# Sending every second-product unit down as fp16 halves in a four-layer attention and mixture kernel

## The chip, the cores and the metric

The program runs on one core of one Trainium2 chip. The metric is device time in microseconds (us) of one execution; three timed executions of the kernel before are given below, and one more execution was profiled.

## The reference

Sixteen samples of 128 rows by 128 features go through four residual layers; each begins with a layer norm (the second and third norms of the list below are of the running `x`).

```python
x = x + _L0_xattn_ref(_layernorm(x), ctx)          # A: softmax(x ctx^T) ctx, one head
x = x + _L0_ffn_ref(_layernorm(x), ...)            # B: 16-head attention, q/k/v weights mixed from 4 experts (top 2)
x = x + _L1_xattn_ref(_layernorm(x), ctx, ...)     # C: 16-head cross attention with rotary positions, 77 keys
x = x + _L1_ffn_ref(_layernorm(x), ...)            # D: causal 16-head attention, then a mixture of 8 experts:
#   y = x + layernorm(attn) * g + b
#   w = softmax over the top 2 of y @ gate_W, spread over 8 experts
#   h = relu(y @ W1[e] + b1[e])        W1[e]: 128 x 512
#   moe = sum_e w[e] * (h @ W2[e] + b2[e])   W2[e]: 512 x 128
#   out = y + layernorm(moe) * g2 + b2'
```

All eight experts are computed for every row and weighted.

## The kernel before

Two samples at a time are a job; there are eight jobs, numbered 0 to 7. A job's layers A to D up to the router run in one of five lanes (jobs 0, 5 in lane 0; 1, 6 in lane 1; 2, 7 in lane 2; 3 and 4 in lanes 3 and 4). The mixtures of experts run in a sixth lane, one job after the other, and a seventh does the splitting of the weights ahead of the first of them. `ORDER` is a string written out by hand of a planner: each digit is a lane that takes its next step, and all five engines walk this one list of steps in this order, each doing its own share of a step. Every engine is thus an in-order queue: an instruction that waits holds up all that stands behind it on its engine. `TAKEN` gives the PSUM bank of each use.

The mixture of a job has 32 units: a unit is 128 of the 4096 hidden columns, four units to an expert. Two units are a piece, so 16 pieces make a job. The step `moe` of piece n does on TensorE the upward product of its two units (three fp16 matmuls each: high weight by high and low input, low weight by high input, L743 to L745), then the downward products of piece n-2 (`down`); on ScalarE two ReLUs of 128x256 from PSUM into the ring `hT` of six units in fp32 (L889). The step `halve` makes fp16 halves of the odd unit alone: VectorE copies `hT` to fp16 (L1108) and GpSimd subtracts to get the low half (L1202); in job 7 (`LATE`) VectorE subtracts too (L1111). Downward, the even unit is multiplied in fp32 (L681) and the odd unit by three fp16 products (L690, L694). Every second expert, `take_up` adds a finished expert's product to `acc`, weighted (L1019).

When a job's mixture is through, VectorE takes moments, GpSimd makes the scales (`moe_end`), ScalarE normalises, GpSimd multiplies and adds twice (`moe_out`, L1213, L1215), and the store goes out. The next job's mixture starts with `moe_start` (L734), which needs that job's router weights: the logits (`D.lg`), six GpSimd instructions that rank them (L1148 to L1155), VectorE's `top`, the transpose `D.cT` (L608) and its copy (L1013). The first product upward needs `ylo` too, which GpSimd makes at the step `top` (L1205).

In each of the 24 attention layers the step `M` finds the maximum of every row and head: four reduces from PSUM into `negmax` (L1088), and after the second sample two more VectorE instructions that split it into an fp16 value and an fp16 remainder, side by side in `m8` (L1092, L1093). The step `mt` turns `m8` by TensorE, and `E` adds it to the scores by a matmul with the constant `two`, which takes up both columns; ScalarE then takes the exponential.

The downward weights of the odd units are split in four parts ahead of job 0: ScalarE copies to fp16 (L854), VectorE subtracts (L1103).

Of the kernel before, what the change touches and what calls it, by code (L numbers as in the profile page):

```python
# [15 lines left out]
NH, HD = 16, 8  # L16
# [5 lines left out]
PARTED = 4  # L22
ODD = E1 * 2
# [50 lines left out]
BANKS, RING, HRING = 8, 8, 6  # L74
# [7 lines left out]
def way(lane):  # L82
# [36 lines left out]
    "2350155215215532055215345452515024525003515551250515454250501205055245054250251450155510520025554025"
    "5105254515522145505250525515205150552551251510522500155521215025015015525255015255521555555015102552"  # L120
    "5555511555251521555255551552155555512515551251552515255555255525555552552555555255255525555555255525"
    "555555555555555555555555555555555555"
# [4 lines left out]
    "0123456701234657012346571023645710236547102536247513062475134067253407125347012653467503412670543126"  # L127
    "7051423670514627054126370514263571406235714056231406523154702631457024635704263157024637102543671025"
    "3741625137425160374265013765041367504163275064130275413027541630725416037251462053174260351432605143"
    "7206513472106347021643567024153670461753046157230461735041273504123650413650416752416572346572347615"  # L130
    "2476152047561340576415736241572431056743107564307562043750621437502143750421650734165047316054173265"
    "4127634127643154273652706432573065417301675041256370142563720164357126435172437521367521607526170562"
# [55 lines left out]
def build(nc, x, ctx, turned, pack, rows, half, w1, w2, b2, out):  # L188
    with ExitStack() as stack:
# [231 lines left out]
        def hi_done(u):  # L421

            return u + 1 + max(0, u - LATE * ODD)

# [4 lines left out]
        def hi_of_w2(n):  # L429
            return w2hi[:, 4 * n:4 * n + 4, :].rearrange("p (a h) d -> p a h d", h=2)  # L430
# [877 lines left out]
```

## Time and profile before

| | us |
|---|---|
| median of 3 runs | 484.89 (484.7 to 485.55) |
| profiled execution, its own time | 483.96 |
| its span, first to last instruction | 481.8 |
| around the span | 2.16 |
| busy: TensorE, VectorE, ScalarE, GpSimd | 441.4, 353.5, 367.0, 236.4 |
| first mixture starts, last one starts | 148.3, 448.6 |

Busy time of TensorE counts each matmul from its start to its modelled end, so overlapping matmuls hide short gaps. The granted clock of TensorE is full speed from 50 us on to the end of the mixtures. In rows of the timeline the first two numbers are the start and the duration in us, and a bracket at the end tells idle time of the engine ahead of it and what ended it.

### The profile page before, as it was taken

The page shows a single profiled execution, that of the slowest core. Times are in us where ns is not written, and L with a number is a line of the kernel's source. Part 1 is how long each engine was busy: PE and PEld are TensorE (multiplying, and loading weights), DVE is VectorE, ACT ScalarE, POOL GpSimd, SP SyncE. Part 2 cuts the span into 40 slices and gives each one's busy share as a digit, 9 for nine tenths or more (in the row PEclk, how much of TensorE's full clock was granted, in tenths as well). Part 3 has the DMA queues.
Part 4 walks back from the last instruction along what each step waited for, and adds up shares of the span by engine and source line. Part 5 has one row for each costly group of instructions (what it writes and reads, how often), then busy time and mean ns, then how long its engine had stood idle before and what let it go on. Part 6 is the DMA issues. An engine that isn't in the chain of part 4 may idle for free.

```text
span 481.8 us, 18999 instructions
## 1 busy us (share of the span) xinstructions
PE 441.4 (92%) x7733; PEld 365.5 (76%) x7733; DVE 353.5 (73%) x1089; ACT 367.0 (76%) x910; POOL 236.4 (49%) x512
## 2 busy tenths in 40 slices
PE   7769888888889999999999999999999999999793
PEld 5536566666667888787888788898798888789693
DVE  3589999888897767697976885769836939456663
ACT  5777788797898887987779778887796586576452
POOL 6763241123226673658454455556535665766402
PEclk8978999999999999999999999999999999999997
DMA  6930000000000000000000000000000000000000
GB/s 193 380 142 1 9 3 10 9 3 3 3 3 14 3 14 2 14 3 7 9 14 3 4 1 3 14 3 1 3 15 2 1 14 2 3 12 1 12 2 12
DMA packets 7949, 11.46 MB, mean 24 GB/s; under 512 B 600, under 2 KB 7224, under 8 KB 7480
## 3 DMA queue, kind: packets, MB, share of 16 engines
q1 hardware_dynamic: 7864, 10.24, 6.5%
q8 instruction: 63, 1.03, 0.9%
q14 instruction: 22, 0.18, 0.1%
HBM read 9.19 MB, written 1.05 MB: 21 GB/s over the span
## 4 chain that ended last, share of the span: by engine, by line
PE 60%; DVE 21%; POOL 9%; issue 4%; ACT 4%; SPq 1%; DMA 0%; POOLq 0%; DVEq 0%; ACTq 0%
PE bk L681 9%; DVE negmax L1088 8%; PE bk L670 6%; PE bk L743 5%; PE bk L690 5%; PE bk L745 4%; PE bk L744 4%; PE bk L656 3%; PE bk L694 3%; PE bk L649 2%; ACT w1f L863 2%; PE bk L626 2%; PE bk L642 2%; PE bk L590 1%; PE bk L596 1%
## 5 line engine op out<-in xcount | busy, mean ns | idle before, releaser
L889 ACT ACTIVATE hT<-bk,pk 128x256 f32<-128x256 f32 x256 | 107.4, 484 | 29.8 <-PE bk L745 29.3
L863 ACT ACTIVATE w1f<-bk 128x512 f32<-128x512 f32 (+1 forms) x192 | 98.8, 601 | 22.4 <-PE bk L656 21.6
L1202 POOL TENSOR_TENSOR w2f<-hT,w2f 128x256 f16<-128x256 f32 x112 | 75.4, 680 | 77.7 <-DVE w2f L1108 77.6
L1088 DVE TENSOR_REDUCE negmax<-bk 128x4 f32<-128x512 f32 (+1 forms) x192 | 105.1, 609 | 10.2 <-PE bk L656 9.6
L681 PE MATMUL bk<-w2f,hT 128*128 128x128 f32 x512 | 79.3, 277 | 0.9 <-ACT hT L889 0.9
L743 PE MATMUL bk<-yhi,w1hi 128*128 128x256 f16 x256 | 70.2, 274 | 0.2 <-DVE qk L1081 0.2
L745 PE MATMUL bk<-yhi,w1lo 128*128 128x256 f16 x256 | 69.8, 273 | 0.0
L744 PE MATMUL bk<-ylo,w1hi 128*128 128x256 f16 x256 | 69.8, 273 | 0.0
L681 PEld LDWEIGHTS bk<-w2f,hT 128*128 128x128 f32 x512 | 67.2, 191 | 3.3 <-ACT hT L889 1.1
L1108 DVE CAST w2f<-hT 128x256 f16<-128x256 f32 x128 | 43.3, 343 | 32.9 <-ACT hT L889 31.8
L670 PE MATMUL bk<-w1f,val 128*32 128x128 f32 (+1 forms) x1536 | 51.5, 275 | 4.5 <-ACT w1f L863 4.5
L656 PE MATMUL bk<-qk 32*128 32x128 f16 (+2 forms) x1536 | 45.4, 213 | 6.1 <-DVE negmax L1088 1.6
L670 PEld LDWEIGHTS bk<-w1f,val 128*32 128x32 f32 (+1 forms) x1536 | 39.4, 109 | 12.0 <-ACT w1f L863 7.0
L656 PEld LDWEIGHTS bk<-qk 32*128 32x128 f16 (+1 forms) x1536 | 32.7, 97 | 13.1 <-issue 9.2
L1019 DVE SCALAR_TENSOR_TENSOR acc<-bk,comb,acc 128x128 f32<-128x128 f32 x128 | 38.3, 340 | 5.7 <-PE bk L694 5.5
L690 PE MATMUL bk<-w2hi,w2f 128*128 128x128 f16 x256 | 42.3, 219 | 0.0
L846 ACT ACTIVATE qk<-bk 128x512 f16<-128x512 f32 x72 | 37.9, 607 | 3.9 <-PE bk L626 3.7
L1137 POOL TENSOR_SCALAR shift<-mv 128x2 f32<-128x2 f32 x40 | 9.4, 235 | 62.7 <-DVE mv L1029 61.1
L694 PE MATMUL bk<-w2hi,w2f 128*128 128x128 f16 x256 | 35.3, 219 | 0.4 <-POOL w2f L1202 0.2
L690 PE MATMUL bk<-w2f 128*128 128x128 f16 x192 | 31.7, 219 | 0.0
L743 PEld LDWEIGHTS bk<-yhi,w1hi 128*128 128x128 f16 x256 | 25.3, 99 | 7.5 <-issue 3.0
L1139 POOL TENSOR_TENSOR rstd<-ve,neghalf 128x2 f32<-128x2 f32 x40 | 28.7, 718 | 3.3
(164 smaller groups left out, 981.9 us busy)
## 6 DMA issues: line engine op xcount, KB each, us to landing
w1f<-in_w SPq DMA_DIRECT2D x1, 2048.0 KB, 14.5
w2f<-in_w SPq DMA_DIRECT2D x1, 2048.0 KB, 17.2
pk<-in_pack SPq DMA_DIRECT2D x1, 1690.0 KB, 7.9
xin<-in_x SPq DMA_DIRECT2D x8, 128.0 KB, 2.4
out<-outb SPq DMA_DIRECT2D x8, 128.0 KB, 1.8
ctxT<-in_turned SPq DMA_DIRECT2D x8, 77.0 KB
cin<-in_ctx SPq DMA_DIRECT2D x8, 77.0 KB
hf<-in_half SPq DMA_DIRECT2D x1, 416.0 KB, 10.1
```

Source lines behind the costliest of these rows:

```text
L656: last = mm(o, qs if q_first else ks, ks if q_first else qs, start=q_first and L != "D", stop=L != "D" or t == NT - 1)
L670: last = mm(o[32 * t:32 * t + 32, (2 * i + a) * T:(2 * i + a + 1) * T], val[s][0:nk, m, SHIFT * r:SHIFT * r + 32], probs[0:nk, ring(n, q), ...
L681: last = mm(o[:, i * D:(i + 1) * D], hT[:, k % HRING, i * T:(i + 1) * T], w2f[:, k, :], start=c == 0 and i == 0, stop=False, skip_group_ch ...
L690: mm(o[:, i * D:(i + 1) * D], hi[:, i * T:(i + 1) * T], w, start=False, stop=False, skip_group_check=True)
L694: last = mm(o[:, i * D:(i + 1) * D], lo[:, i * T:(i + 1) * T], w2hi[:, k // 2, :], start=False, stop=c == CH - 1, skip_group_check=True)
L743: mm(o[:, m * W:(m + 1) * W], hi, yhi[s][:], start=True, stop=False)
L744: mm(o[:, m * W:(m + 1) * W], hi, ylo[s][:], start=False, stop=False)
L745: last = mm(o[:, m * W:(m + 1) * W], lo, yhi[s][:], start=False, stop=True)
L863: act.activation(probs[0:nk, ring(n, q), :], bank(g, st, q)[0:nk, :], ACT.Exp, scale=SCALE[L]).then_inc(s_exp, 1)
L889: act.activation(hT[:, k % HRING, :], bank(g, st)[:, m * W:(m + 1) * W], ACT.Relu, bias=P("b1")[:, k:k + 1]).then_inc(s_relu, 1)
L1088: dve.tensor_reduce(negmax[s][:, i, NT * q:NT * (q + 1)], bank(g, st, q)[:, 0:NT * nk].rearrange("p (t k) -> p t k", t=NT), X_AXIS, ALU.ma ...
L1202: pool.tensor_tensor(hlo(u), hT[:, k % HRING, :], hhi(u), ALU.subtract).then_inc(s_hlo, 1)
```

## The change

- Every unit, even ones too, goes down by three fp16 products (high by high, high by low weight, low by high weight); the fp32 product is gone.
- `halve` makes both units' halves: VectorE copies the high halves of a piece by one instruction of 512 columns, which waits for both ReLUs, and GpSimd subtracts twice, 256 columns each. In job 7 GpSimd subtracts the first unit's and VectorE the second's.
- `hT` holds four units and not six; a ReLU waits until the low half of the unit that lay there is made (`lo_done`), and no longer for the product downward. Halves of six units (three pieces) are kept; the copy waits for the products downward of three pieces ago. The two ReLUs of a piece are done first unit first.
- All of the downward weights are split, in eight parts of 512 columns, over the fp32 ones: ScalarE copies, GpSimd (no longer VectorE) subtracts.
- The reduces of `M` write the fp16 value into `m8` at once; `negmax`, L1092 and L1093 go, the remainder with them, and `two` takes up one column. The matmul of `mt` waits for the reduces themselves.
- `ORDER` and `TAKEN` are written anew. Ahead of the first `moe_start` stand 257 steps (252 before); the number of `M` steps ahead of each `moe_start` is as before. What changes at the last two borders of jobs, read out of the two strings (the digit is the lane, the mixture's own steps without one):

```
job 5 to 6, before: ... moe 13 | halve 13 | 1 D.lg | 2 E 0 | moe 14 | 1 top | halve 14 | moe 15 | 2 PV 0 | halve 15 | 1 D.cT | moe_end | 2 E 1 | moe_out | store | moe_start
job 5 to 6, after:  ... moe 15 | halve 15 | 1 D.lg | 2 E 0 | moe_end | 2 PV 0 | 1 top | 2 E 1 | 1 D.cT | moe_out | store | moe_start
job 6 to 7, before: ... 2 D.yT | moe 11 | halve 11 | 2 D.lg | moe 12 | ... | moe 14 | halve 14 | moe 15 | 2 top | halve 15 | moe_end | moe_out | 2 D.cT | store | moe_start
job 6 to 7, after:  ... moe 14 | halve 14 | moe 15 | 2 D.yT | halve 15 | 2 D.lg | moe_end | 2 top | moe_out | store | 2 D.cT | moe_start
```

The diff, without the two strings, the allocation of semaphores and of `negmax`, and blank lines:

```diff
@@ -19,8 +19,7 @@
 SPLITS = 8
-PARTED = 4
-ODD = E1 * 2
+PARTED = 8
 LATE = 7
@@ -71,7 +70,7 @@
 BIASED = ("B", "D")
-BANKS, RING, HRING = 8, 8, 6
+BANKS, RING, HRING = 8, 8, 4
 STACK_DVE = (1,)
@@ -283,8 +281,8 @@
         hT = sb("hT", [128, HRING, W])
-        w2hi = sb("w2hi", [128, ODD, D], F16)
-        w2lo0 = sb("w2lo0", [128, ODD // PARTED, D], F16)
+        w2x = sb("w2x", [128, 2, 2, CH, D], F16)
+        hx = sb("hx", [128, 2, 2, W], F16)
         acc = sb("acc", [128, SPS, D])
@@ -418,34 +415,29 @@
             return {"A": xin[s], "B": xs[s], "C": xs[s], "D": xs[s], "D2": on[s]}[N]
-        def hi_done(u):
-            return u + 1 + max(0, u - LATE * ODD)
-        def odd_of_w2(n):
-            return w2f[:, 8 * n:8 * n + 8, :].rearrange("p (a h x) d -> p a h x d", h=2, x=2)[:, :, :, 1, :]
-        def hi_of_w2(n):
-            return w2hi[:, 4 * n:4 * n + 4, :].rearrange("p (a h) d -> p a h d", h=2)
-        halves = w2f[:].rearrange("p u d -> p (u d)").bitcast(F16).rearrange("p (u d) -> p u d", d=2 * D)
-        def hhi(u):
-            return halves[:, 13 + 4 * (u % (HRING // 2)), :]
-        def hlo(u):
-            return halves[:, 15 + 4 * (u % (HRING // 2)), :]
-        def lo_of_w2(n):
-            if n == 0:
-                return w2lo0[:].rearrange("p (a h) d -> p a h d", h=2)
-            return halves[:, 4 * n - 3:4 * n:2, :].rearrange("p a (h d) -> p a h d", h=2)
-        def lo_of_unit(k):
-            n, m = k // 8, k % 8 // 2
-            return w2lo0[:, m, :] if n == 0 else halves[:, 4 * n - 3 + 2 * (m // 2), m % 2 * D:(m % 2 + 1) * D]
+        def hi_done(n):
+            return n + 1 + max(0, n - LATE * PIECES)
+        def lo_done(g, n, m):
+            if g < LATE:
+                return s_hlo, 2 * n + m + 1
+            return (s_hhi, hi_done(n) + 1) if m else (s_hlo, LATE * PIECES + n + 1)
+        halves = w2f[:].rearrange("p u d -> p (u d)").bitcast(F16).rearrange("p (n w) -> p n w", n=PARTED)
+        def part_of_w2(n):
+            return w2f[:, CH * n:CH * (n + 1), :]
+        def split_w2(n):
+            return w2x[:, n] if n < 2 else halves[:, n - 2, :].rearrange("p (x c d) -> p x c d", x=2, c=CH)
+        def split_h(n):
+            q = n % 3
+            return hx[:] if q == 2 else halves[:, PARTED - 2 + q, :].rearrange("p (m x w) -> p m x w", m=2, x=2)
         def part_of_w1(n):
@@ -580,7 +572,7 @@
                 elif h.endswith("mt"):
-                    pe.wait_ge(s_m8[s], layer(g, h[0]))
+                    pe.wait_ge(s_mred, NQ * (NUMBER[g, ("M", s, h[0], SPS - 1)] + 1))
                     half_bank = o[:].bitcast(F16)
@@ -675,23 +667,16 @@
                 o = take_bank(pe, j, *emptied(e)) if c == 0 else products(j, e)
-                if k % 2 == 0:
-                    pe.wait_ge(s_relu, j * UNITS + k + 2)
-                    for i in range(SPS):
-                        last = mm(o[:, i * D:(i + 1) * D], hT[:, k % HRING, i * T:(i + 1) * T], w2f[:, k, :],
-                                  start=c == 0 and i == 0, stop=False, skip_group_check=True)
-                    last.then_inc(s_down, 1)
-                    return
-                u = j * ODD + k // 2
-                hi, lo = hhi(u), hlo(u)
-                pe.wait_ge(s_hhi, hi_done(u))
+                n, m = j * PIECES + k // 2, k % 2
+                h, w = split_h(n)[:, m], split_w2(e)[:, :, c, :]
+                pe.wait_ge(s_hhi, hi_done(n))
                 for i in range(SPS):
-                    for w in (w2hi[:, k // 2, :], lo_of_unit(k)):
-                        mm(o[:, i * D:(i + 1) * D], hi[:, i * T:(i + 1) * T], w, start=False, stop=False,
-                           skip_group_check=True)
-                pe.wait_ge(*((s_hhi, hi_done(u) + 1) if j >= LATE else (s_hlo, u + 1)))
+                    for x in range(2):
+                        mm(o[:, i * D:(i + 1) * D], h[:, 0, i * T:(i + 1) * T], w[:, x, :],
+                           start=c == 0 and i == 0 and x == 0, stop=False, skip_group_check=True)
+                pe.wait_ge(*lo_done(j, n, m))
                 for i in range(SPS):
-                    last = mm(o[:, i * D:(i + 1) * D], lo[:, i * T:(i + 1) * T], w2hi[:, k // 2, :],
+                    last = mm(o[:, i * D:(i + 1) * D], h[:, 1, i * T:(i + 1) * T], w[:, 0, :],
                               start=False, stop=c == CH - 1, skip_group_check=True)
@@ -728,7 +713,7 @@
                         pe.wait_ge(s_w1lo, SPLITS)
-                        pe.wait_ge(s_w1lo, SPLITS + PARTED)
+                        pe.wait_ge(s_w2lo, PARTED)
                     pe.wait_ge(s_read[s], read(g // LANES, "D.cT"))
@@ -851,7 +836,8 @@
                     act.wait_ge(s_moe, N_MOE * 16)
-                    act.activation(hi_of_w2(st[2]), odd_of_w2(st[2]), ACT.Copy).then_inc(s_w1hi, 1)
+                    after(act, s_w2lo, st[2] - 1)
+                    act.activation(split_w2(st[2])[:, 0], part_of_w2(st[2]), ACT.Copy).then_inc(s_w2hi, 1)
                 elif kind == "E":
@@ -883,9 +869,11 @@
                     act.wait_ge(s_up, NUMBER[g, st] + 1)
-                    for m in (1, 0):
+                    for m in range(2):
                         k = 2 * st[2] + m
-                        after(act, s_down, g * UNITS + k + 1 - HRING)
+                        before = g * PIECES + st[2] - HRING // 2
+                        if before >= 0:
+                            act.wait_ge(*lo_done(before // PIECES, before, m))
                         act.activation(hT[:, k % HRING, :], bank(g, st)[:, m * W:(m + 1) * W], ACT.Relu,
@@ -1085,31 +1073,22 @@
                     for q in range(NQ):
-                        dve.tensor_reduce(negmax[s][:, i, NT * q:NT * (q + 1)], bank(g, st, q)[:, 0:NT * nk].rearrange(
+                        dve.tensor_reduce(m8[s][:, i, NT * q:NT * (q + 1), 0], bank(g, st, q)[:, 0:NT * nk].rearrange(
                             "p (t k) -> p t k", t=NT), X_AXIS, ALU.max, negate=True).then_inc(s_mred, 1)
-                    if i == SPS - 1:
-                        dve.wait_ge(s_mred, NQ * (n + 1))
-                        link(dve.tensor_copy(m8[s][:, :, :, 0], negmax[s][:]))
-                        dve.tensor_tensor(m8[s][:, :, :, 1], negmax[s][:], m8[s][:, :, :, 0], ALU.subtract
-                                          ).then_inc(s_m8[s], 1)
                 elif kind == "split":
...
                     dve.tensor_tensor(w1lo[:, piece], w1f[:, piece], w1hi[:, piece], ALU.subtract).then_inc(s_w1lo, 1)
-                elif kind == "part":
-                    n = st[2]
-                    dve.wait_ge(s_w1hi, SPLITS + n + 1)
-                    dve.wait_ge(s_w1lo, SPLITS + n)
-                    dve.tensor_tensor(lo_of_w2(n), odd_of_w2(n), hi_of_w2(n), ALU.subtract).then_inc(s_w1lo, 1)
                 elif kind == "halve":
-                    k = 2 * st[2] + 1
-                    u = g * ODD + st[2]
-                    dve.wait_ge(s_relu, g * UNITS + k)
-                    dve.tensor_copy(hhi(u), hT[:, k % HRING, :]).then_inc(s_hhi, 1)
+                    n = g * PIECES + st[2]
+                    r = 2 * st[2] % HRING
+                    dve.wait_ge(s_relu, 2 * n + 2)
+                    after(dve, s_down, 2 * n - 4)
+                    dve.tensor_copy(split_h(n)[:, :, 0, :], hT[:, r:r + 2, :]).then_inc(s_hhi, 1)
                     if g >= LATE:
-                        dve.wait_ge(s_hhi, hi_done(u))
-                        dve.tensor_tensor(hlo(u), hT[:, k % HRING, :],
-                                          hhi(u), ALU.subtract).then_inc(s_hhi, 1)
+                        dve.wait_ge(s_hhi, hi_done(n))
+                        dve.tensor_tensor(split_h(n)[:, 1, 1, :], hT[:, r + 1, :], split_h(n)[:, 1, 0, :], ALU.subtract
+                                          ).then_inc(s_hhi, 1)
                 elif kind == "hop":
@@ -1195,12 +1174,16 @@
                     pool.tensor_tensor(base[s][:], xy[s], rows_of("b2"), ALU.add).then_inc(s_base[s], 1)
-                elif kind == "halve" and g < LATE:
-                    k = 2 * st[2] + 1
-                    u = g * ODD + st[2]
-                    pool.wait_ge(s_hhi, u + 1)
-                    pool.tensor_tensor(hlo(u), hT[:, k % HRING, :], hhi(u),
-                                       ALU.subtract).then_inc(s_hlo, 1)
+                elif kind == "part":
+                    n = st[2]
+                    pool.wait_ge(s_w2hi, n + 1)
+                    pool.tensor_tensor(split_w2(n)[:, 1], part_of_w2(n), split_w2(n)[:, 0], ALU.subtract).then_inc(s_w2lo, 1)
+                elif kind == "halve":
+                    n = g * PIECES + st[2]
+                    pool.wait_ge(s_hhi, hi_done(n))
+                    for m in range(2 if g < LATE else 1):
+                        pool.tensor_tensor(split_h(n)[:, m, 1, :], hT[:, (2 * st[2] + m) % HRING, :],
+                                           split_h(n)[:, m, 0, :], ALU.subtract).then_inc(s_hlo, 1)
                 elif kind == "top" and st[2] == "D":
@@ -1252,7 +1235,7 @@
     for t in range(NT):
-        two[(rows_ // 8 % 4 == t) & (rows_ % 8 < 2), t] = 1.0
+        two[(rows_ // 8 % 4 == t) & (rows_ % 8 < 1), t] = 1.0
     half = {"ident16": np.eye(128, dtype=np.float16), "lowS": np.tile(lowS, (4, 1)),
```

## Rows read from the trace of the kernel before

**Rows 1.** The page: busy time of each engine, and the chain that ended last by engine.

```profile
PE 441.4 (92%) x7733; PEld 365.5 (76%) x7733; DVE 353.5 (73%) x1089; ACT 367.0 (76%) x910; POOL 236.4 (49%) x512
...
PE 60%; DVE 21%; POOL 9%; issue 4%; ACT 4%; SPq 1%; DMA 0%; POOLq 0%; DVEq 0%; ACTq 0%
```

**Rows 2.** Windows: stretch, length, busy us of TensorE, its loads, VectorE, ScalarE, GpSimd, clock.

```profile
50.00:100.00 50.00, 42.34 (x925) 31.03 (x921) 45.86 (x119) 41.56 (x97) 12.94 (x33) 1.00 0.03 8
...
148.00:196.00 48.00, 47.36 (x828) 39.82 (x830) 36.14 (x128) 39.68 (x104) 26.31 (x59) 1.00 0.03 8
...
386.00:424.00 38.00, 36.73 (x647) 32.21 (x646) 22.12 (x66) 26.85 (x66) 23.82 (x43) 1.00 0.02 6
424.00:449.00 25.00, 23.26 (x253) 21.66 (x251) 15.66 (x52) 14.13 (x36) 16.49 (x31) 1.00 0.02 7
```

**Rows 3.** Timeline of TensorE, one piece of job 7.

```profile
456.89 0.61 PE L681 MATMUL bk<-w2f,hT 128*128 128x128 f32 x4
...
457.34 0.22 PE L690 MATMUL bk<-w2hi,w2f 128*128 128x128 f16 x1
...
457.68 0.27 PE L743 MATMUL bk<-yhi,w1hi 128*128 128x256 f16 x1
...
458.33 0.61 PE L681 MATMUL bk<-w2f,hT 128*128 128x128 f32 x4
```

**Rows 4.** Groups by shape: busy us, mean ns of one, idle time before.

```profile
L1202 POOL TENSOR_TENSOR w2f<-hT,w2f 128x256 f16<-128x256 f32 x112 | 75.4, 680 | 77.7 <-DVE w2f L1108 77.6
...
L1093 DVE TENSOR_TENSOR m<-negmax,m 128x32 f16<-128x32 f32 x24 | 7.3, 304 | 0.8
...
L1092 DVE CAST m<-negmax 128x32 f16<-128x32 f32 x24 | 6.3, 262 | 0.8
...
L854 ACT ACTIVATE w2hi<-w2f 128x512 f16<-128x512 f32 x4 | 2.6, 644 | 0.0
L1103 DVE TENSOR_TENSOR w2f<-w2f,w2hi 128x512 f16<-128x512 f32 x3 | 2.1, 689 | 0.3 <-ACT w2hi L854 0.3
```

**Rows 5.** One line's instructions: shortest, median and longest of one, ns.

```profile
L1108 DVE CAST w2f<-hT x128: 259/291/818, 150.9 to 472.0; 128x256 f16<-128x256 f32 x128
...
L1111 DVE TENSOR_TENSOR w2f<-hT,w2f x16: 424/426/899, 452.1 to 472.3; 128x256 f16<-128x256 f32 x16
```

**Rows 6.** Timeline of GpSimd in job 5.

```profile
407.60 1.57 POOL L1202 TENSOR_TENSOR w2f<-hT,w2f 128x256 f16<-128x256 f32 x2 [0.23 <-DVE w2f L1108]
...
412.20 0.54 POOL L1148 TENSOR_TENSOR qkf<-lg 128x64 f32<-128x64 f32 x2
...
415.23 0.67 POOL L1205 TENSOR_TENSOR ylo<-qk,yhi 128x256 f16<-128x256 f32 x1
416.82 1.30 POOL L1202 TENSOR_TENSOR w2f<-hT,w2f 128x256 f16<-128x256 f32 x2 [0.93 <-DVE w2f L1108]
```

**Rows 7.** Timeline of VectorE beside the first of rows 6.

```profile
407.74 0.89 DVE L1056 TENSOR_TENSOR wc<-wc,rw 128x256 f32<-128x256 f32 x1
```

**Rows 8.** Timeline of GpSimd in job 6: its first and last of 16 subtractions.

```profile
424.36 0.67 POOL L1202 TENSOR_TENSOR w2f<-hT,w2f 128x256 f16<-128x256 f32 x1
...
445.93 0.67 POOL L1202 TENSOR_TENSOR w2f<-hT,w2f 128x256 f16<-128x256 f32 x1 [0.31 <-DVE w2f L1108]
```

**Rows 9.** Timeline of TensorE at the last two borders of jobs.

```profile
421.62 1.08 PE L670 MATMUL bk<-w1f,val 128*32 128x128 f32 x32 [0.93 <-ACT w1f L863]
...
448.61 0.69 PE L734 MATMUL bk<-b2f,combT 16*128 16x256 f32 x2 [1.56 <-DVE combT L1013]
449.24 0.28 PE L743 MATMUL bk<-yhi,w1hi 128*128 128x256 f16 x1
```

**Rows 10.** Timeline of VectorE at the border of jobs 6 and 7.

```profile
444.16 0.27 DVE L926 TENSOR_REDUCE rank<-qkf 128x16 f32<-128x128 f32 x1
...
445.45 0.20 DVE L949 TENSOR_TENSOR comb<-picked,lmax 128x16 f32<-128x16 f32 x1
...
448.31 0.25 DVE L1013 COPY combT<-bk 16x128 f32<-16x128 f32 x1
```

More of the change, by code:

```diff
@@ L119 @@
[L119 to L122, printed above, removed]
+    "0100132012041041320410210320140302414126034601066600124006642612401010243121300241032024103020132062"
+    "1104261401320401230261014021201314620163420160132410140410120304420312340123060123123024103101213310"
@@ new lines @@
+    "1431042101342310340132431032400310202361042310243201102235515235511452530541525531525401501554023255"
+    "1035501555035554512550515025015321053215550340451052124530502014305525351525514503352150245352001524"
+    "3310501235254155010514251535254515524501254450315505204555531022450552351525532510524035203515205314"
+    "5312052515215521523055124545531255052342530054515515525105250545054020515051250550245052540522155125"
+    "4005150525545124505525125052515525015505215515250152250012151205505155525052255011552551255555521051"
@@ L123 @@
+    "0525555155155552255251555151555255155251551555555512521215555552555555555225555255525555555555552525"
+    "2552555555555555555555555555555555555555"
 )
 TAKEN = (
[L127 to L130, printed above, removed]
@@ L136 @@
-    "6032175460213745620173462051374260513746201534760213"
+    "0123456701234567012345607134265071342560713421536042715360452371604523160452317604523147562031457620"
+    "3146527013465021534620513647250132645071324650732476503247160532741607534167053241607532640713526740"
+    "1352645013425670314257603145760341576034215736047213504671354067312540673152470361572403617241036724"
+    "5103567240135624031526754032167540251467042561370452176042317604215604231526034572605347120547120457"
+    "1360247130621473526134527164035271654037165470135470213457620134570123647012360475230647520364713526"
@@ L137 @@
+    "4572134571234157236015723601576213456241630241760352417603451207364152731645214735621475210475201654"
+    "2015426301542367154236715432670543627025740361576401527164527162453071642507416250712653012365012764"
+    "5071264510673415207314527031653270651372657163457163452763045217632014756314275031427540127534016534"
+    "0615734021573460157342015723406457203165240321765402176542176504247653021765402167530241756324017536"
+    "4051736420157642310567432150643271506437120653742015"
 )
@@ L318, in build @@
         s_hl = per_lane(sem, "s_hl")
-        s_m8 = per_lane(sem, "s_m8")
         s_bias = per_lane(sem, "s_bias")
@@ L332, in build @@
         s_up, s_relu, s_down = sem("s_up"), sem("s_relu"), sem("s_down")
-        s_hhi, s_hlo = sem("s_hhi"), sem("s_hlo")
+        s_hhi, s_hlo, s_w2hi, s_w2lo = sem("s_hhi"), sem("s_hlo"), sem("s_w2hi"), sem("s_w2lo")
         s_accinit, s_acc = sem("s_accinit"), sem("s_acc")
```

11 lines of the change are left out of this document (removed).

## The prediction

> **What bounds the kernel now.** I read the page first. TensorE is busy 92% of the span and makes up 60% of the chain that ended last, VectorE 21%, GpSimd only 9%; GpSimd is busy 49% [rows 1]. The windows say that this is an average over three different kernels. Ahead of the first mixture (50 to 100 us) VectorE is the fullest, 45.9 of 50 us, with TensorE and ScalarE near 42 [rows 2]. From 148 us on TensorE is busy in 97% and more of nearly every stretch, VectorE and ScalarE in 60 to 85%, GpSimd in 55% (26.3 of 48). Toward the end, when fewer lanes are left to fill in, GpSimd's share climbs: 23.8 of 38 us in job 5, 16.5 of 25 in job 6 [rows 2]. Then the timelines. A piece in job 7 starts every 1.44 us on TensorE (456.89 to 458.33): the fp32 unit takes 0.45, the fp16 unit 0.34, the upward products 0.65, with nothing between [rows 3]. So a mixture alone is bound by TensorE; what GpSimd does there now (one subtraction of 0.68 for each piece [rows 4]) fits easily.
>
> **The change, part by part.**
>
> *The fp32 unit becomes an fp16 one.* 0.45 becomes 0.34 [rows 3], so 0.11 us for each of 128 pieces, 14.1 us of TensorE: 1.76 in each job. It is the largest gain, and worth something only where TensorE sets the pace. In jobs 0 to 4 (80 pieces, 8.8 us) the bounds are nothing and 8.8; I take the chain's share of TensorE, 60% [rows 1]: **-5.3**.
>
> *The maxima and the split of the weights.* L1092 and L1093 cost 0.26 + 0.30 = 0.57 us of VectorE for each of 24 layers [rows 4], between the last reduce and the transpose that waits for it. Ten layers pass ahead of the first mixture: 5.7 us. The four subtractions L1103 that leave VectorE are 4 x 0.69 = 2.8 [rows 4]. Against that stand four more copies on ScalarE, 4 x 0.64 = 2.6 [rows 4], and eight subtractions of 512 columns on GpSimd: L1202 has 256 in 0.68, so between 0.68 and 1.36 each; I take the upper end, 10.9 us, hidden, as GpSimd is busy in 12.9 of 50 us there [rows 2]; without that cover the first mixture would be late by them. Bounds: 8.5 gained, 1 lost if ScalarE becomes the tightest. VectorE is the fullest of three nearly full engines, so I take about half: **-4**. The other 14 layers (8 us) lie where VectorE has idle time beside a full TensorE: nothing, and at most 1.6 by VectorE's 21% of the chain.
>
> *The copy of 512 columns.* A copy of 256 has a median of 0.29 us; VectorE's subtraction takes 0.426 for 256 and 0.689 for 512, so 1.03 ns a column [rows 4, 5]. The copy's rate isn't shown by two sizes. Below: 0.29, if it were all fixed; above: 0.29 + 256 x 1.03 ns = 0.56. I take the middle, 0.42. That is 128 x 0.13 = 17 us of VectorE, covered by its idle 16 of 38 us in job 5 and 9 of 25 in job 6 [rows 2]. It now waits for the second ReLU of its piece as well; the product downward that needs it comes two pieces later, over 2.6 us at 1.33 each, and hides that.
>
> *The second subtraction.* 128 more on GpSimd (112 in jobs 0 to 6, 16 in job 7). Back to back two take 1.30 to 1.31, so 0.65 each [rows 6]: 83 us, and with the split's 11 GpSimd goes from 236 to about 330, 69% of the span. In jobs 0 to 4 this makes some 37 of 48 us for each, still under TensorE; I charge nothing beyond the 60% above. In the last two jobs it isn't under TensorE, and this is where I look for the answer.
>
> *What two such instructions do to VectorE and the reverse.* In rows 6 two subtractions at 407.60 take 1.57 us and not 1.30. Beside them VectorE ran an addition with both inputs in SBUF, at 407.74, which took 0.89 [rows 7]; VectorE's own subtraction of that size takes 0.426 alone, and up to 0.899 [rows 5]. They take turns: VectorE waited for the first subtraction to end, and the second was put off by 0.27. The copy shows the same spread, 0.259 to 0.818 [rows 5]. With two subtractions in each piece GpSimd is always in the way of the next copy, so I charge 0.27 for each piece: a piece costs GpSimd 1.30 + 0.27 = 1.57 us, against TensorE's new 1.44 - 0.11 = 1.33. Bounds: 1.30, if the copy falls into a gap; 1.30 + 0.42 = 1.72, if the copy holds GpSimd for all its length.
> The Trainium skill ("SBUF — State Buffer", section "Who interferes with whom") states that VectorE in its two-port mode, or with two SBUF inputs, and GpSimd share a port pair that is locked for the whole instruction. The trace agrees that they take turns, but shows 0.27 of delay where the whole instruction would be 0.43; by the page's rule the piece would be 1.72, and the sum that of the second rival below.
>
> *The new waits.* A ReLU waits for the low half of two pieces ago, and behind it on ScalarE are queued the next ReLUs and the lanes' evictions and exponentials, for which TensorE waits. TensorE itself needs that same low half for the product downward that follows in its queue, so where GpSimd is in time the wait costs nothing, and where it is late the loss is already in GpSimd's pace for a piece. The copy's wait for the products of three pieces ago is past by then: TensorE does those one piece earlier.
>
> *Job 5* (386 to 424): GpSimd 23.8 + 16 x 0.65 = 34.2 of 38 [rows 2, 6], but its ranks (412.20 to 415.23, 3.0 us) and `ylo` move behind the last piece. TensorE would save 1.8; I take **-0.5** (bounds -1.8 and +1.5).
>
> *Job 6.* From its first subtraction to the end of its last it has 22.2 us (424.36 to 446.60) [rows 8]. Afterwards: 16 x 1.57 = 25.1, and what else GpSimd does in that stretch: 16.5 of busy time less 16 x 0.68, less ranks 3.0 and `ylo` 0.7, which move behind it, leaves 1.9 [rows 2, 4, 6]. 27.0 against 22.2: **+4.8** (bounds: -1.8 at TensorE's pace, +7.2 at 1.72).
>
> *The border of jobs 6 and 7.* Before, the router of lane 2 is worked out beside pieces 11 to 15, and the first upward product of job 7 starts 2.6 us after the last subtraction (446.60 to 449.24) [rows 8, 9]. Afterwards `D.lg` is queued behind piece 15, so GpSimd ranks after its last subtraction, 3.0 [rows 6]; VectorE's `top` takes 1.5 (444.16 to 445.65) [rows 10]; the transpose, its copy and `moe_start` 0.6 + 0.65 (the copy at 448.31 lies 0.30 ahead of L734, the transpose I take as much, L734 to L743 0.63) [rows 9, 10]. 5.8 against 2.6: **+3.2**, nothing if GpSimd has run dry by then. The other things queued there (scales, `ylo`) are done by 5.3, so they don't come last.
> *The border of 5 and 6* has the same new order, and there TensorE has one product of probabilities and values more in between (421.62, 1.0 us [rows 9]): **+2.2** (bounds 0 and 3.2).
>
> *Job 7.* GpSimd has one subtraction for each piece and VectorE the other: 0.65 + 0.27 + 0.27 of turns stay below TensorE's 1.33. 16 x 0.11 = 1.8 gained, less some turns: **-1.5** (bounds -1.8, +1.3).
>
> Sum: -4 - 5.3 - 0.5 + 2.2 + 4.8 + 3.2 - 1.5 = -1.1. The profiled execution took 483.96 (481.8 and 2.16 around it), so 482.9 by it; it lies 0.9 below the median of the runs, so I say **483.8**.
>
> **Rivals.**
> *GpSimd stays hidden.* The copies fall into gaps, and TensorE keeps the pace everywhere: jobs 0 to 4 -8.8, jobs 5 to 7 -1.8 each, start -4, while the borders keep +2.2 and +3.2, as the order is fixed: -12.8, **472.1**. For it: GpSimd's idle time before the subtractions is 77.7 us, all of it waiting for the copy [rows 4], so as a whole there is room. Against it: in job 6 even 16 x 1.30 + 1.9 = 22.7 is more than the 22.2 of now.
> *Slower: the copy locks GpSimd for all of its 0.42.* Then a piece costs 1.72, job 6 +7.2 in place of +4.8, and in job 7 the turns are 0.42 + 0.43 + 0.65 = 1.50 for each piece, 16 x (1.50 - 1.44) = +1.0 in place of -1.5. That is +4.9 on the sum: +3.8, **488.7**. For it: copies of up to 0.818 and subtractions up to 0.899 [rows 5]. Against it: the 0.27 of rows 6 and 7. By job 6 alone the sign turns where its piece costs 1.57 + 1.1/16 = 1.64.
>
> **How the numbers follow.** The forecast has 0.5, with a range of its own of 479.5 to 487.5 (the start 0 to 8.5 and jobs 0 to 4 0 to 8.8, which will hardly err the same way); GpSimd hidden 0.2; the lock 0.3. A measurement of this kernel can tell about 0.2%, 1.0 us. Forecast: 0.27 faster, 0.14 within, 0.09 slower, as its centre is just past the edge; the first rival adds 0.2 to faster, the second 0.02 to within and 0.28 to slower: 0.47, 0.16, 0.37. Low end: half of the first rival, 474; high end: the lock with a start that gains nothing much, 490.
>
> **What would show it.** Right: a piece in job 6 every 1.5 to 1.65 us, with GpSimd busy over 90% and TensorE idle in each; in job 7 every 1.33; over 5 us from the last subtraction of job 6 to the first upward product of job 7; the first mixture at about 144. Wrong: a piece of 1.35 in job 6 (rival one), of 1.7 (rival two), or a first mixture no earlier; and above all if jobs 0 to 4 together shorten by less than 3 or by more than 9, since there I only took a share.

## The result: 3% slower

The changed kernel takes 499.9 us (498.77 to 500.47, 4 runs), the kernel before 485.11 beside it: ratio 1.0301, 95% interval 1.0285 to 1.0318. The profiled execution took 500.47, its span is 498.7. The forecast was 483.8, in a range up to 490.

The page after (busy time and chain by engine; compare [rows 1]):

```profile
PE 440.3 (88%) x7989; PEld 354.4 (71%) x7989; DVE 361.3 (72%) x1037; ACT 373.6 (75%) x914; POOL 342.2 (69%) x648
...
PE 38%; POOL 24%; DVE 20%; ACT 9%; issue 7%; DMA 0%; POOLq 0%; DVEq 0%
```

GpSimd has 106 us more to do and 24% of the chain (9 before); TensorE fell from 60 to 38%. Where the time went is read from the start of each job's mixture (first record of the `b2f` matmul, us from the span's start; the last column is the span):

| job | 0 | 1 | 2 | 3 | 4 | 5 | 6 | 7 | end |
|---|---|---|---|---|---|---|---|---|---|
| before | 148.3 | 195.2 | 246.0 | 300.7 | 344.7 | 385.5 | 419.3 | 448.6 | 481.8 |
| after | 151.7 | 194.3 | 252.1 | 306.4 | 351.2 | 393.3 | 431.0 | 465.3 | 498.7 |
| after is late by | 3.4 | -0.9 | 6.0 | 5.7 | 6.4 | 7.9 | 11.7 | 16.7 | 16.9 |

Between the first mixture and the start of job 5 the rows of single jobs can't be compared: only at the starts of jobs 5, 6 and 7 have the two orders done the same steps (but for the four more parts of the split). At that of job 1 the new order is seven steps behind, at those of jobs 2 to 4 one or two ahead. So: 3.4 late at the first mixture, 4.4 more by the end of job 4, 3.9 in job 5, 5.0 in job 6, 0.2 in job 7.

The windows after (columns as in [rows 2]; the stretches are about jobs 0, 5 and 6 and most of 7):

```profile
148.00:196.00 48.00, 45.21 (x842) 37.11 (x838) 36.88 (x121) 37.90 (x101) 38.75 (x76) 0.98 0.03 8
...
393.00:431.00 38.00, 33.56 (x627) 27.86 (x628) 23.95 (x66) 26.57 (x63) 33.55 (x57) 1.00 0.02 6
431.00:465.00 34.00, 27.20 (x333) 22.31 (x333) 17.03 (x53) 18.19 (x43) 32.61 (x53) 0.98 0.02 5
465.00:490.00 25.00, 24.23 (x282) 21.17 (x282) 16.92 (x47) 14.58 (x35) 17.77 (x21) 0.89 0.03 7
```

In job 0 GpSimd is busy 38.8 of 48 us and TensorE 45.2, so TensorE is still the fuller one; in job 6 GpSimd is busy 32.6 of 34, TensorE 27.2. In the stretch of job 7 the mean granted clock (the eighth figure) falls to 0.89. The timeline of GpSimd in job 6, whose last subtraction ends at 460.2, with the first ranking instruction behind it:

```profile
449.97 2.98 POOL L1185 TENSOR_TENSOR w2f<-hT,w2f 128x256 f16<-128x256 f32 x4 [0.37 <-DVE w2f L1087]
452.90 1.53 POOL L1185 TENSOR_TENSOR hx<-hT,hx 128x256 f16<-128x256 f32 x2
454.40 3.03 POOL L1185 TENSOR_TENSOR w2f<-hT,w2f 128x256 f16<-128x256 f32 x4
...
458.88 1.30 POOL L1185 TENSOR_TENSOR w2f<-hT,w2f 128x256 f16<-128x256 f32 x2
460.14 0.54 POOL L1127 TENSOR_TENSOR qkf<-lg 128x64 f32<-128x64 f32 x2
```

Two subtractions start every 1.5 us; with no copy beside them the last two take 1.26 to the next instruction (458.88 to 460.14). In job 7, where VectorE takes one of the two, a piece on TensorE takes 1.33 (compare [rows 3], 1.44):

```profile
475.69 0.39 PE L675 MATMUL bk<-w2f,hx 128*128 128x128 f16 x4
...
477.02 0.39 PE L675 MATMUL bk<-w2f 128*128 128x128 f16 x4
```

The border of jobs 6 and 7 on TensorE (compare [rows 9]):

```profile
460.50 0.28 PE L679 MATMUL bk<-w2f 128*128 128x128 f16 x2
464.55 0.37 PE L600 MATMUL bk<-pk,comb 128*16 128x128 f32 x1 [3.77 <-DVE comb L937]
465.29 1.22 PE L719 MATMUL bk<-b2f,combT 16*128 16x256 f32 x2 [0.37 <-DVE combT L1001]
466.44 0.39 PE L728 MATMUL bk<-yhi,w1hi 128*128 128x256 f16 x1
466.62 0.42 PE L729 MATMUL bk<-ylo,w1hi 128*128 128x256 f16 x1
466.84 0.42 PE L730 MATMUL bk<-yhi,w1lo 128*128 128x256 f16 x1
```

TensorE waits 3.8 us for the ranks and VectorE's `top` behind them, and then starts an upward matmul every 0.21 us, not every 0.107 as in job 6. The granted clock is at its lower level (1.2 GHz of 2.4) from 463.7 to 470.5:

```profile
463.80:470.50 6.70, 5.58 (x24) 3.46 (x25) 2.06 (x7) 2.95 (x8) 5.29 (x8) 0.50 0.07 20
```

### The profile page after: what moved, and what is told of

It reads as the page before. It is cut to its first block, busy times and chain, and to the rows that moved or that the text cites. A ratio compares the mean times of both kernels' runs of the same rounds, so it can differ in the third digit from the quotient of the medians.

```text
span 498.7 us, 19729 instructions
## 1 busy us (share of the span) xinstructions
PE 440.3 (88%) x7989; PEld 354.4 (71%) x7989; DVE 361.3 (72%) x1037; ACT 373.6 (75%) x914; POOL 342.2 (69%) x648
## 4 chain that ended last, share of the span: by engine, by line
PE 38%; POOL 24%; DVE 20%; ACT 9%; issue 7%; DMA 0%; POOLq 0%; DVEq 0%
POOL w2f L1185 8%; DVE m L1076 8%; PE bk L662 5%; ACT w1f L849 5%; POOL hx L1185 4%; PE bk L675 4%; PE bk L728 3%; PE bk L648 3%; PE bk L730 2%; PE bk L729 2%; PE bk L679 2%; POOL rstd L1118 2%; PE bk L641 2%; ACT hT L877 2%; PE bk L522 2%
## 5 line engine op out<-in xcount | busy, mean ns | idle before, releaser
L877 ACT ACTIVATE hT<-bk,pk 128x256 f32<-128x256 f32 x256 | 110.1, 480 | 38.2 <-PE bk L730 28.6
L1185 POOL TENSOR_TENSOR w2f<-hT,w2f 128x256 f16<-128x256 f32 x161 | 115.0, 736 | 27.6 <-DVE w2f L1087 27.6
L1076 DVE TENSOR_REDUCE m<-bk 128x4 f16<-128x512 f32 (+1 forms) x192 | 105.3, 617 | 7.7 <-PE bk L648 7.3
L1087 DVE CAST w2f<-hT 128x512 f16<-128x512 f32 x86 | 41.6, 484 | 31.0 <-ACT hT L877 30.9
L1185 POOL TENSOR_TENSOR hx<-hT,hx 128x256 f16<-128x256 f32 x79 | 55.1, 716 | 7.3 <-DVE hx L1087 7.3
L662 PE MATMUL bk<-w1f,val 128*32 128x128 f32 (+1 forms) x1536 | 53.4, 281 | 3.0 <-ACT w1f L849 2.9
L662 PEld LDWEIGHTS bk<-w1f,val 128*32 128x32 f32 (+1 forms) x1536 | 40.4, 112 | 11.3 <-ACT w1f L849 4.3
L1116 POOL TENSOR_SCALAR shift<-mv 128x2 f32<-128x2 f32 x40 | 11.9, 298 | 51.3 <-DVE mv L1017 49.5
L675 PE MATMUL bk<-w2f 128*128 128x128 f16 x512 | 46.6, 219 | 0.0
L679 PE MATMUL bk<-w2f 128*128 128x128 f16 x256 | 35.5, 220 | 5.8 <-POOL w2f L1185 4.4
L1087 DVE CAST hx<-hT 128x512 f16<-128x512 f32 x42 | 22.3, 530 | 24.6 <-ACT hT L877 24.4
L675 PEld LDWEIGHTS bk<-w2f 128*128 128x128 f16 x512 | 36.1, 98 | 1.7 <-ACT yhi L805 0.3
```

The source lines that it names most:

```text
L662: last = mm(o[32 * t:32 * t + 32, (2 * i + a) * T:(2 * i + a + 1) * T], val[s][0:nk, m, SHIFT * r:SHIFT * r + 32], probs[0:nk, ring(n, q), ...
L675: mm(o[:, i * D:(i + 1) * D], h[:, 0, i * T:(i + 1) * T], w[:, x, :], start=c == 0 and i == 0 and x == 0, stop=False, skip_group_check=True)
L679: last = mm(o[:, i * D:(i + 1) * D], h[:, 1, i * T:(i + 1) * T], w[:, 0, :], start=False, stop=c == CH - 1, skip_group_check=True)
L877: act.activation(hT[:, k % HRING, :], bank(g, st)[:, m * W:(m + 1) * W], ACT.Relu, bias=P("b1")[:, k:k + 1]).then_inc(s_relu, 1)
L1076: dve.tensor_reduce(m8[s][:, i, NT * q:NT * (q + 1), 0], bank(g, st, q)[:, 0:NT * nk].rearrange("p (t k) -> p t k", t=NT), X_AXIS, ALU.max ...
L1087: dve.tensor_copy(split_h(n)[:, :, 0, :], hT[:, r:r + 2, :]).then_inc(s_hhi, 1)
```

## The experiments

Theory: the added load on GpSimd costs the time, in all jobs, not only where GpSimd is full. Rivals: the new order of steps; the new waits (a ReLU for the low half, a ring of four); VectorE's wider copy. Each time stands beside runs of the kernel before on the same chip; those differ by 0.4 us at most between the chips, so that runs of different rows can be compared as well.

| run | us | before | ratio, 95% interval |
|---|---|---|---|
| e1_one_sub | 485.66 | 485.2 | 1.0008 (0.9990 to 1.0025) |
| e2_old_order | 517.94 | 485.2 | 1.0701 (1.0648 to 1.0753) |
| e3_late0 | 507.19 | 485.2 | 1.0458 (1.0428 to 1.0489) |
| e4_before_plus_sub | 516.47 | 485.2 | 1.0645 (1.0598 to 1.0693) |
| e5_before_maxima | 482.27 | 484.79 | 0.9948 (0.9933 to 0.9962) |
| e6_sub_behind | 505.80 | 484.79 | 1.0435 (1.0414 to 1.0457) |
| e7_fill_border | 499.09 | 484.79 | 1.0289 (1.0266 to 1.0312) |
| e8_wide_sub | 501.79 | 484.79 | 1.0378 (1.0340 to 1.0416) |
| e9_fp16_down_alone | 480.50 | 484.92 | 0.9901 (0.9871 to 0.9930) |
| e10_reduce_copy | 495.50 | 484.92 | 1.0210 (1.0181 to 1.0239) |
| e11_early_rank | 506.17 | 484.92 | 1.0445 (1.0411 to 1.0479) |
| e12_one_copy_one_sub | 482.20 | 485.09 | 0.9945 (0.9922 to 0.9967) |
| e13_before_plus_copy | 502.65 | 485.09 | 1.0366 (1.0337 to 1.0394) |

**The second subtraction left out (e1).** The waits are counted to match.

```diff
-                    for m in range(2 if g < LATE else 1):
+                    for m in (1 if g < LATE else 0,):
```

> The changed kernel with GpSimd's subtraction for the even unit left out in jobs 0 to 6 (the odd unit's low half is multiplied in its place, so the mixture's result is not the reference's); order, copies, products and rings as changed. If GpSimd's second subtraction is what costs: GpSimd busy falls from 342 to about 262 us, and the time from 499.9 to 470 to 477. If the new order of steps costs: 495 or more. If the wait of the ReLU on the low half costs by its length alone, something between, with GpSimd idle and ScalarE waiting for it.

485.66: 14.2 us won, GpSimd at 264. So this subtraction is nearly the whole loss, but the 470 to 477 was missed: without it the kernel only stands where it stood, though TensorE has 14 us less to do by the forecast's count. That gap is taken up below. Jobs 0 to 4 together take 234.9 us (149.8 to 384.7) and not 241.6 (151.7 to 393.3): 6.7 of the 14.2 are lost in jobs for which the forecast charged GpSimd nothing.

**The old order under the changed instructions (e2).** The strings `ORDER` and `TAKEN` of before, each of the four old parts followed by a new one.

> The changed kernel with the order of steps and of banks of before (the four more parts of the split each stand beside one of the old four). If GpSimd's load is what costs: 496 to 503, with the pace of a piece in job 6 at 1.5 us again. If the new order costs: 484 to 489, the first mixture at 148 and jobs 5 and 6 back at 34 and 29 us.

517.94, 18 us slower than with the new order: both expectations missed, and the rival fell the other way. The new order is what keeps the loss at 15. A piece in job 6 takes 1.5 us here too (four subtractions in 3.03).

**VectorE takes half of the subtractions in every job (e3).**

```diff
-LATE = 7
+LATE = 0
```

> The changed kernel with LATE = 0: in every job GpSimd subtracts the first unit's half and VectorE the second's, as in job 7. 112 subtractions of 0.43 go to VectorE (361 to about 409 us busy), GpSimd falls to about 265. If GpSimd's load is what costs: 476 to 486, below the kernel before if VectorE stays under TensorE. If VectorE becomes the bound in its place: 490 to 500. If the order costs: 497 or more.

507.19. GpSimd falls to 286, VectorE rises to 404, and the time rises by 7: load moved from one engine to the other costs there as well. Neither 476 to 486 nor 490 to 500 was met; the number fits "497 or more", but the order is not what costs, as the run before this one shows.

**The load alone, on the kernel before, ahead of the real subtraction (e4) and behind it (e6).**

```diff
+                    link(pool.tensor_tensor(filler[:], hT[:, k % HRING, :], hhi(u), ALU.subtract))   # e4
                     pool.tensor_tensor(hlo(u), hT[:, k % HRING, :], hhi(u),
                                        ALU.subtract).then_inc(s_hlo, 1)
+                    link(pool.tensor_tensor(filler[:], pk[:, 0:256], w1hi[:, 0:256], ALU.subtract))  # e6
```

> The kernel before with one more subtraction of the same size on GpSimd ahead of each of its 112, into a buffer that nobody reads: the load alone, without the order, the rings, the copies or the products of the change. If GpSimd's load is what costs: 492 to 500, most of it in jobs 5 and 6 where GpSimd fills. If it is the order or the waits: 485 to 488.

> The kernel before with one more GpSimd subtraction of the same size for each of the 112, this time behind the real one, from constants into a buffer that nobody reads. Against the run that put it ahead (+31 us): if that loss was the low half coming later to TensorE, only 0 to 12 us remain; if it is what is queued behind on GpSimd (scales, ranks, the next low half), 22 to 32 us remain.

516.47 and 505.8: 31 and 21 us. The first is well above the 492 to 500 expected, the second just under the 22 to 32. The page with the subtraction ahead:

```profile
PE 454.5 (88%) x7733; PEld 370.2 (72%) x7733; DVE 364.8 (71%) x1089; ACT 367.8 (71%) x910; POOL 312.9 (61%) x624
...
PE 38%; POOL 27%; DVE 23%; issue 6%; ACT 4%; DMA 0%; POOLq 0%; DVEq 0%
```

76.5 us more on GpSimd, which is then busy only 61% (66 to 75% in each of jobs 0 to 4), cost 31. By jobs it is 3.7, 4.1, 4.2, 3.3, 4.0, 5.0, 6.6, 1.2 (starts 150.7, 201.3, 256.4, 315.2, 362.5, 407.2, 446.0, 482.0, end 516.4): the early jobs, where GpSimd has idle time, lose nearly as much as the late ones. About two thirds remain when no other engine waits for the added instruction itself: they are lost to what is queued behind it on GpSimd. The traces show where a part of it goes. These are TensorE's products with the low half in the kernel before, in e4 and in e6; the last figures are its idle time ahead of them and who ended it:

```profile
L694 PE MATMUL bk<-w2hi,w2f 128*128 128x128 f16 x256 | 35.3, 219 | 0.4 <-POOL w2f L1202 0.2
...
L694 PE MATMUL bk<-w2hi,w2f 128*128 128x128 f16 x256 | 35.7, 221 | 18.2 <-POOL w2f L1203 17.7 <-DVE negmax L1088 0.3
...
L694 PE MATMUL bk<-w2hi,w2f 128*128 128x128 f16 x256 | 35.8, 222 | 6.5 <-POOL w2f L1202 6.2
```

So TensorE waits 17.7 us for the low half in e4 and 6.2 in e6, against 0.2. Which instructions pass on the rest (the scales, the ranks) was not taken apart.

**The maxima alone (e5).** The kernel before with the reduces writing into `m8`.

> The kernel before with the change of the maxima alone: the reduces write fp16 into the operand of the transpose, 48 VectorE instructions (0.57 us for each of 24 layers) go, order and mixture as before. If the removed instructions lie on the path ahead of the first mixture, as the prediction had it: 3 to 5 us faster, with the first mixture at 144 to 146. If TensorE and ScalarE are as full as VectorE there: within 1 us of before.

482.27: 2.5 us faster than before, under the 3 to 5 expected, and the fastest version here that computes all of the reference. The first mixture starts at 148.1 against 148.3: in these two profiles the gain comes afterwards. The start itself scatters by more (148.3 to 150.7 in the runs that have the instructions and the order of before up to there: before, e4, e6, e9, e13).

**The fp16 products alone (e9)**, with the odd unit's halves for both:

```diff
-                if k % 2 == 0:
-                    ...   # fp32 product
-                    return
+                    for x, w in enumerate((w2hi[:, k // 2, :], lo_of_unit(k | 1))):
```

> The kernel before with the change of the downward product alone: the even units go down by three fp16 products too, but with the halves of the odd unit and of its weights, so that nothing more is copied or subtracted (the mixture's result is not the reference's). TensorE has 14.1 us less to do. If its saving reaches the end as the prediction had it (60% in jobs 0 to 4, nearly all in 5 to 7): 9 to 13 us faster. If the engines' waits for each other hold the pace with the old order: 0 to 5 us faster.

480.5: 4.4 of the 14.1 us reach the end (0.6, 0.7, 0.3, 0.7, 0.7 in jobs 0 to 4). TensorE's busy time falls by 12.0 (441.4 to 429.4).

**One more copy on VectorE, alone (e13); and the change with neither copy nor subtraction added (e12).**

```diff
+                    link(dve.tensor_copy(filler[:], hT[:, k % HRING, :]))                            # e13, on the kernel before
-                    dve.tensor_copy(split_h(n)[:, :, 0, :], hT[:, r:r + 2, :]).then_inc(s_hhi, 1)    # e12
+                    dve.tensor_copy(split_h(n)[:, 1, 0, :], hT[:, r + 1, :]).then_inc(s_hhi, 1)
```

> The kernel before with one more copy of 256 columns on VectorE ahead of each of its 128 (of the same unit, into a buffer that nobody reads), 0.29 us and a wait for its end each: the load of the wider copy and more, without the rest. If VectorE's load in the mixtures costs as GpSimd's does: 8 to 20 us slower. If it is hidden in VectorE's idle time, as the prediction had it: 0 to 3 us.

> The changed kernel with all added work on VectorE and GpSimd in the mixtures left out: only the odd unit is copied (256 columns) and subtracted, and the even unit goes down with its halves (the mixture's result is not the reference's). What remains of the change are the fp16 products, the rings and waits, the split weights, the maxima and the new order. If the copy of 512 columns is what holds the run without the second subtraction at 485.7: 477 to 481, the sum of the two parts tried alone on the kernel before (-2.5 and -4.8). If the order or the ring of four units holds it: 483 to 487.

Forty us more on VectorE (353.5 to 393.9) cost 17.6; here, as in e4, the real copy waits behind the added one, and no run put it behind. The change with neither, at 482.2, fell between its two ranges. Without the added copy the run without the second subtraction falls from 485.7 to 482.2, so the wider copy costs 3.5 on the new order (with GpSimd's 16 subtractions of job 7, which are left out here too). The two parts alone would make 478; some 4 us stay with the new order, its ring or the lower clock, and are not settled. No run took the ring of four, or the ReLU's wait for the low half, by itself; in the profile after, ScalarE's ReLUs wait 7.8 us for low halves:

```profile
L877 ACT ACTIVATE hT<-bk,pk 128x256 f32<-128x256 f32 x256 | 110.1, 480 | 38.2 <-PE bk L730 28.6 <-POOL w2f L1185 6.5 <-POOL hx L1185 1.3
```

**The turns.** Two subtractions as one instruction of 512 columns (e8); and the copy of jobs 5 and 6 as a reduce (e10).

```diff
+                        pool.tensor_tensor(split_h(n)[:, :, 1, :], hT[:, r:r + 2, :], split_h(n)[:, :, 0, :],
+                                           ALU.subtract).then_inc(s_hlo, 1)                          # e8
+                        dve.tensor_reduce(split_h(n)[:, :, 0, :], hT[:, r:r + 2, :].unsqueeze(3), X_AXIS, ALU.max
+                                          ).then_inc(s_hhi, 1)                                      # e10
```

> The changed kernel with GpSimd's two subtractions of a piece made by one instruction of 512 columns in jobs 0 to 6. By the split's instruction of that size, 1.16 us, against two at 1.25 to 1.30, GpSimd is busy some 14 us less and takes one turn with VectorE for each piece, not two. If GpSimd's load is what costs: 4 to 9 us faster than the changed kernel (491 to 496), a piece of job 6 at 1.35 to 1.45. If the wait for a low half costs by its length: no gain, as the even unit's half comes 0.5 us later.

> The changed kernel with the high halves of jobs 5 and 6 copied by a reduce over an axis of one element, which has one input in SBUF and runs at one column a cycle (about 0.6 us for 512). If the copy of 512 and GpSimd's subtractions take turns for a port, and that turn sets the pace of 1.49 us a piece in job 6: the reduce runs beside them, and a piece falls to 1.30 to 1.35, 4 to 6 us in all (494 to 496). If the pace comes from GpSimd's own two instructions or from the wait for the copy: 1.5 still, and no gain.

GpSimd and VectorE's copy in job 6 with the wide subtraction; then the same with the reduce; and last a copy of the changed kernel in job 6:

```profile
452.86 1.16 POOL L1186 TENSOR_TENSOR hx<-hT,hx 128x512 f16<-128x512 f32 x1 [0.36 <-DVE hx L1087]
453.46 0.83 DVE L1087 CAST w2f<-hT 128x512 f16<-128x512 f32 x1 [0.17 <-ACT hT L877]
454.37 1.15 POOL L1186 TENSOR_TENSOR w2f<-hT,w2f 128x512 f16<-128x512 f32 x1 [0.36 <-DVE w2f L1087]
```

```profile
441.60 2.55 POOL L1189 TENSOR_TENSOR w2f<-hT,w2f 128x256 f16<-128x256 f32 x4
...
445.19 0.67 DVE L1088 TENSOR_REDUCE w2f<-hT 128x512 f16<-128x512 f32 x1
445.94 2.56 POOL L1189 TENSOR_TENSOR w2f<-hT,w2f 128x256 f16<-128x256 f32 x4
448.54 1.30 POOL L1189 TENSOR_TENSOR hx<-hT,hx 128x256 f16<-128x256 f32 x2
```

```profile
453.49 0.43 DVE L1087 CAST w2f<-hT 128x512 f16<-128x512 f32 x1 [0.55 <-ACT hT L877]
```

The wide one is shorter, 1.16, but each piece still takes 1.51: the copy of the next piece, begun at 453.46 beside it, takes 0.83 and not 0.43 and ends only after it (454.02), and GpSimd waits 0.36 for it. 24 us less on GpSimd gained nothing (501.79, not 491 to 496), so the sheer load is not all. By its time alone this run can't tell the turn from the other expectation, the later half of the even unit; its rows show the turn, and the reduce decides. With the reduce, which takes 0.67 and not 0.43, the four subtractions of two pieces take 2.55 and not 2.98 to 3.03, and two pieces follow each other in 2.60: no turn. Job 6 falls from 34.3 to 31.8 us, job 5 from 37.7 to 36.4, the time to 495.5, as expected. So the turn costs 4.4 us in these two jobs.

The Trainium skill ("SBUF — State Buffer", section "Who interferes with whom") says that on this chip a reduce never contends with GpSimd while a copy in two-port mode locks the pair; both runs agree on who waits. The delay that the copy adds to two subtractions is 0.24 (1.50 against 1.26), though, not the 0.43 of the whole copy.

**The border.** Idle matmuls where TensorE waits for the ranks (e7); and the last two routers put back beside the pieces (e11, a change of the two strings alone).

```diff
                 elif h == "D.cT":
+                    if LANES * g + s == JOBS - 1:
+                        fill(o, 36)
```

> The changed kernel with 36 idle matmuls of 128x256 fp16 put into TensorE's queue ahead of the last transpose of router weights, where TensorE waits for the ranks between jobs 6 and 7. If the half clock of 462 to 472 us comes from that wait and costs job 7 its gain: the clock stays full there, and 1 to 3 us are won (497 to 499). If the clock fell because of the gaps in job 6 ahead of it, it falls again, and nothing is won.

> The changed kernel with the last two routers put back where they stood before: transposes, logits, ranks and weights of job 7 beside pieces 11 to 15 of job 6, those of job 6 beside the last pieces of job 5. GpSimd's work is the same. If the border costs 3 us each because the ranks stand behind the last subtraction: job 6 grows by the ranks' 3 us and the border shrinks by as much, TensorE doesn't fall to half clock, and 1 to 4 us are won. If GpSimd's load alone sets the time of job 6 and its border: nothing changes by more than 1 us.

With the idle matmuls the clock stays full and job 7 takes 32.7 us, not 33.4: 0.7 us in the profile, too little for the timing to show (499.09, the intervals overlap). With the routers put back it is 6.3 us worse, outside both expectations: jobs 5, 6 and 7 take 41.0, 36.5 and 36.3. The new order of these two borders is thus worth about a third of the 18 us of e2. The last subtraction of job 6, the start of job 7 and TensorE's longest waits for a low half around it:

```profile
460.31 0.28 PE L679 MATMUL bk<-w2f 128*128 128x128 f16 x2 [2.08 <-POOL w2f L1185]
464.40 1.29 POOL L1185 TENSOR_TENSOR w2f<-hT,w2f 128x256 f16<-128x256 f32 x2
468.72 0.39 PE L728 MATMUL bk<-yhi,w1hi 128*128 128x256 f16 x1
474.27 0.28 PE L679 MATMUL bk<-w2x,w2f 128*128 128x128 f16 x2 [1.78 <-POOL w2f L1185]
```

The gap from the last subtraction to the first upward product shrinks to 3.0 us (465.7 to 468.7), but TensorE waits 2.1 us behind the ranks in job 6, and 1.8 in job 7 behind the scales and the output of job 6 and two more additions, which GpSimd here does ahead of job 7's first subtraction. The granted clock also falls to its lower level three times for 3.4 us from 461 on; what each of these costs was not taken apart.

## Why the prediction was wrong

The step that failed is in the part on the second subtraction: "In jobs 0 to 4 this makes some 37 of 48 us for each, still under TensorE; I charge nothing". In the change's own order that subtraction costs 6.7 us in these five jobs and 14.2 in all (e1). The copy, "covered by its idle" time, costs 2.3 there and 3.5 in all (e1 against e12). With neither, jobs 0 to 4 are 4.6 us shorter than before (e12; the maxima and the new order are in this): -4.6 + 2.3 + 6.7 makes the +4.4 that was measured, where -5.3 was forecast. The prediction's own sign of being wrong, jobs 0 to 4 shortening by less than 3, came true. The two rivals charge nothing for these jobs either.

Of the 18.0 us between the forecast's sum (-1.1) and the profile (+16.9), jobs 0 to 4 make 9.7, the start 7.4, job 5 2.2 and job 7 1.7; job 6 came out 3.0 better. Point by point, by its own steps:

- **Jobs 0 to 4, -5.3: wrong, it was +4.4**, by the step above. The other step, "I take the chain's share of TensorE, 60%", was too high on the old order: the saving alone passes 3.0 of 8.8 us there, 34% (e9). In the new order it can't be told from the maxima.
- **The start, -4: not seen.** The maxima give 2.5 us in all (e5). The runs with the same instructions and order as the changed kernel up to there (e1, e3, e7, e8, e10, e11, e12) start the first mixture at 148.5 to 150.7, the profile after at 151.7, so most of its 3.4 us is scatter. Part of that may be the clock: its granted clock is at the lower level at 95.1 to 98.5 and 146.3 to 149.7, in before at full speed there; the three runs that don't fall ahead of the first mixture (e3, e7, e11) start it at 148.5 to 148.8. The new order also has one more step `M` ahead of the first mixture (21, 20 before), against what the list of changes says.
- **The copy "covered by its idle" time: wrong**, as said above. Its length of 0.42 was right (0.43).
- **A piece in job 6, 1.57: near** (1.50, GpSimd busy 96%), with the mechanism that was given, the turns (e8, e10). From the first subtraction to the end of the last it takes 25.8 us (434.3 to 460.2), 27.0 was forecast. It is the reason for the late jobs only.
- **The border of 6 and 7, +3.2: near.** The first upward product starts 6.3 us after the last subtraction (460.2 to 466.4), 5.8 was forecast, and the ranks come last as it said. But the loss is not the order's: with the ranks where they were before, this gap is 3.0 again and the kernel is 6.3 us slower (e11).
- **Jobs 5 and 6 with their borders** were forecast at +9.7 and came to +8.9, in part by luck: job 5 at +1.7 came to +3.9, job 6 at +8.0 to +5.0.
- **Job 7, -1.5: right in its pace, 1.33, wrong in its time** (+0.2): the lower clock after the wait took about 0.7 of it (e7). The rest of the miss was not taken apart.

On the old order the parts can be added up as well: fp16 products -4.4, maxima -2.5, the second subtraction +31.3 (e4), the copies (128 of them 63.9 us after, 43.3 before, so 20.6 at e13's 17.6 for 40.4) +9.0: +33.4, where the changed instructions on the old order measured +32.7 (e2). This is no proof of the split: with e6's 21.0 for the subtraction the sum would be 23.1, and the copies' price is scaled from a run with one wait more. The new order takes back 18. What the prediction lacked is such a price: it asked of each engine whether it was full, and not what a us of it passes on.

## What to carry to other kernels

Where all engines walk one order of steps, an engine's queue can hand delay on though it is not full: here 74 to 76.5 us added to GpSimd cost 21 to 31 us of time, 40 us added to VectorE 17.6, and 14.1 us taken from TensorE, the busiest engine at 92%, gave 4.4. Before moving work from the busiest engine to an idle one, put the load alone on the idle one and time that: an edit of one line would have told the sign here. Of this change the maxima are worth keeping by themselves (482.3 us, 0.5% faster).

## What the runs showed of the hardware

A VectorE copy of fp32 to fp16 in SBUF and a GpSimd subtraction take turns, and joining two subtractions into one does not help: the copy waits for the longer one (1.50 against 1.51 us a piece). The same copy as a reduce over one element is 0.24 us longer by itself (0.67 against 0.43) and runs beside GpSimd (two pieces in 2.60, e10). A GpSimd subtraction of 512 columns takes 1.16 us (e8), two of 256 one behind the other 1.26. And TensorE, at full clock from 149.7 us to 463.7 in the profile after, ran its next matmuls at half the rate after the wait of 3.8 us at the end of job 6, until 470.5 (0.21 us each, not 0.107); with 36 idle matmuls in that wait the granted clock stayed full (e7).
